# Second-layer routed output products as three float32r terms of high and low parts, in a two-layer transformer kernel

## What is computed

```python
def _L1_ffn_ref(hidden_states, router_w, w_gate_up, w_down, shared_gate_up, shared_down):
    ...
    router_logits = x @ router_w.T
    topk_vals, topk_ids = jax.lax.top_k(router_logits, top_k)      # top_k = 1, 8 experts
    gate = jax.nn.sigmoid(topk_vals.astype(jnp.float32)).astype(x.dtype)
    xs = (x[:, None, :] * gate[:, :, None]).reshape(-1, d)
    def body(acc, inp):
        wg, wd, e = inp
        h = _silu_mul(xs @ wg)                                     # silu(g) * u, each 512 wide
        o = h @ wd
        mask = (ids_flat == e)[:, None]
        return (acc + jnp.where(mask, o, jnp.zeros((), o.dtype)), None)
    ...
    shared = _silu_mul(x @ shared_gate_up) @ shared_down
    return (routed + shared).reshape(b, s, d)
```

## Time and profile before

| | |
|---|---|
| median of 3 runs | 1307.61 us (1305.98 to 1308.95) |
| the profiled execution | 1313.01 us |
| its span in the profile | 1311.2 us |
| granted TensorE clock, mean | 0.982 |
| TensorE busy | 1252.6 us (96%) |
| TensorE weight loads | 1079.0 us |
| VectorE, ScalarE, GpSimd busy | 688.8, 538.8, 668.5 us |

### The profile page before, as it was taken

One profiled execution on the slowest core, in us unless ns is written; L12 is line 12 of the kernel. 1 busy time (PEld: TensorE's weight loads), 2 busy tenths in 40 slices (PEclk: granted clock), 3 DMA queues, 4 the chain that ended last, 5 costly groups with the idle time before them and its releaser, 6 DMA issues. The chain is left out here.

```text
span 1311.2 us, 21675 instructions
## 1 busy us (share of the span) xinstructions
PE 1252.6 (96%) x7877; PEld 1079.0 (82%) x7877; DVE 688.8 (53%) x1423; ACT 538.8 (41%) x1190; POOL 668.5 (51%) x523
## 2 busy tenths in 40 slices
PE   6688999999999998999999999999999999999999
PEld 5467888888867887888788888888888887899988
DVE  6994555555676567675645434444333333433235
ACT  3675666665565333334333334333343333311122
POOL 3645778876202554576767664765545553021110
PEclk9798999999998999999999999999999999999999
DMA  9624888886705211121221112111111102799931
GB/s 317 160 53 97 175 176 183 181 176 129 177 1 161 69 53 52 61 65 49 77 69 62 36 53 69 53 38 63 53 53 36 37 25 68 273 334 336 334 126 65
DMA packets 112698, 150.70 MB, mean 115 GB/s; under 512 B 12145, under 2 KB 94193, under 8 KB 112465
## 3 DMA queue, kind: packets, MB, share of 16 engines
q1 hardware_dynamic: 96320, 123.21, 29.6%
q0 software_dynamic: 16272, 26.10, 10.5%
HBM read 121.31 MB, written 27.97 MB: 114 GB/s over the span
## 5 line engine op out<-in xcount | busy, mean ns | idle before, releaser
L1630 PE MATMUL a_p_p<-a_xr,a_wr 128*128 128x512 f32 x1152 | 308.7, 403 | 2.4 <-DVE g_x L2190 2.4
L1630 PEld LDWEIGHTS a_p_p<-a_xr,a_wr 128*128 128x128 f32 x1152 | 206.6, 189 | 42.7 <-DVE g_x L2190 3.1
L1957 POOL TENSOR_TENSOR a_sqsum<-a_sqsum,a_sq 128x512 f32<-128x512 f32 x60 | 77.8, 1297 | 232.5 <-ACT a_sq L1839 232.5
L1925 POOL TENSOR_TENSOR a_wr<-g_hold,a_wr 128x768 fp32r<-128x768 f32 x63 | 122.3, 1942 | 20.2 <-DVE a_wr L1989 20.2
L2025 DVE SCALAR_TENSOR_TENSOR a_gated<-a_th,a_p_o 128x512 f32<-128x512 f32 x64 | 44.0, 688 | 159.1 <-ACT a_sq L1839 159.1
L410 POOL DMA_INDIRECT acc<-l_ye,g_slot_token x64 | 104.5, 1632 | 39.7 <-ACT l_ye L777 19.7
L1959 POOL TENSOR_TENSOR a_gr<-a_gated,a_gr 128x512 fp32r<-128x512 f32 x64 | 97.8, 1528 | 23.7 <-DVE a_gr L2029 23.7
L1643 PE MATMUL a_p_p<-a_wvr,a_xr 128*128 128x512 f32 x384 | 108.8, 421 | 0.8 <-DVE a_xr L1983 0.8
L1701 PE MATMUL a_p_w<-a_gr,l_wo_r 128*128 128x512 f32 x384 | 100.8, 397 | 0.3 <-POOL a_gr L1959 0.3
L1685 PE MATMUL a_p_o<-a_sc,a_v 128*128 128x128 f32 x512 | 89.9, 278 | 6.6 <-DVE a_sc L2005 6.6
L1812 ACT ACTIVATE a_qk<-a_p_p 128x512 f32<-128x512 f32 x64 | 38.2, 597 | 141.0 <-PE a_p_p L1630 141.0
(11 more groups left out here) (292 smaller groups left out, 2790.7 us busy)
## 6 DMA issues: line engine op xcount, KB each, us to landing
g_hold<-in_Wqkg SPq DMA_DIRECT2D x64, 384.0 KB, 3.2
e_up<-in_gate_up SPq DMA_DIRECT2D x23, 1024.0 KB, 7.4
g_hold<-in_gate_up SPq DMA_DIRECT2D x64, 192.0 KB
e_down<-in_down SPq DMA_DIRECT2D x23, 512.0 KB, 5.9
g_hold<-in_Wv SPq DMA_DIRECT2D x16, 512.0 KB, 4.3
l_down<-in_down SPq DMA_DIRECT2D x64, 96.0 KB
acc<-l_zero SPq DMA_DIRECT2D x2, 2176.0 KB, 12.7
rows<-l_zero SPq DMA_DIRECT2D x1, 2955.5 KB, 26.9
```

The source lines that it names most:

```text
L1630: mm = pe.matmul(dst[:, :], wr[n % 2][:, wp, kk, c * P:(c + 1) * P], xr[n // H1 % 2][:, xp, kk, :], start=(kk, xp, wp) == (0, 0, 0), stop= ...
L1925: pool.tensor_tensor(wr[n % 2][:, 1, :, :], w[n % 2], wr[n % 2][:, 0, :, :], ALU.subtract).then_inc(w_parts, 1)
L1957: pool.tensor_tensor(sqsum[b % 2][:, :], sqsum[b % 2][:, :], sq[a % 2][:, :], ALU.add).then_inc(summed, 1)
```

## The change

The routed tiles' output product is computed in the three terms too.

- `hT` becomes a pair of float32r buffers, high and low, for each of its two places. VectorE writes the product of SiLU and up product to `prod`, ScalarE copies it to the high part (`high_hidden`), VectorE subtracts for the low part.
- `down` of each tile is split into `dr`, which lies in `sT[1]`, half of it for even and half for odd tiles. ScalarE makes the high part (`high_part`), GpSimd the low part (`low_part`). Both wait for the output product of tile t - 2, which read that half before.
- `output` has 12 instructions with float32r operands in place of 4 products in float32 (8 instructions), and waits for `part_low` instead of for `down`'s load.
- The shared unit of group 1 waits until the last routed output products have read `sT[1]`.

```diff
-        hT = [m.sb(f"hT{s}", [P, HC, P]) for s in range(2)]
+        hT = [[m.sb(f"hT{s}{i}", [P, HC, P], F32R) for i in range(2)] for s in range(2)]
...
+        dr = [[sT[1][i][:, 2 * s:2 * s + 2, :].rearrange("p a (b n) -> p (a b) n", n=D) for i in range(2)] for s in (1, 0)]
...
         @block.gpsimd
         def _(pool):
+            def low_part(t):
+                pool.wait_ge(part_high, t + 1)
+                if t >= 2:
+                    pool.wait_ge(y_done, Y["r", t - 2, 0] + 1)
+                pool.tensor_tensor(dr[t % 2][1], down[t % WR][:, :, :], dr[t % 2][0], ALU.subtract).then_inc(part_low, 1)
+
+            low_part(0)
             for t in range(RT1):
+                if t + 1 < RT1:
+                    low_part(t + 1)
                 pool.wait_ge(y_kept, Y["r", t, 0] + 1)
...
             def output(t):
                 y = Y["r", t, 0]
                 pe.wait_ge(h_ready, U["r", t, 0] + 1)
-                pe.wait_ge(down_in[t % WR], 16 * (t // WR + 1))
+                pe.wait_ge(part_low, t + 1)
                 pe.wait_ge(y_kept, y - 2)
-                for c in range(HC):
-                    mm = pe.matmul(p_y[y % 3][:, 0:D], hT[t % 2][:, c, :], down[t % WR][:, c, :], start=c == 0, stop=c == HC - 1)
+                terms = list(itertools.product(range(HC), ((0, 0), (0, 1), (1, 0))))
+                for n, (c, (a, b)) in enumerate(terms):
+                    mm = pe.matmul(p_y[y % 3][:, 0:D], hT[t % 2][a][:, c, :], dr[t % 2][b][:, c, :], start=n == 0, stop=n == len(terms) - 1)
                 mm.then_inc(y_done, 1)
...
+            def high_part(t):
+                act.wait_ge(down_in[t % WR], 16 * (t // WR + 1))
+                if t >= 2:
+                    act.wait_ge(y_done, Y["r", t - 2, 0] + 1)
+                act.activation(dr[t % 2][0], down[t % WR][:, :, :], ACT.Copy).then_inc(part_high, 1)
+
+            def high_hidden(u, t):
+                act.wait_ge(prod_ready, u + 1)
+                if t >= 2:
+                    act.wait_ge(y_done, Y["r", t - 2, 0] + 1)
+                act.activation(hT[t % 2][0][:, :, :].rearrange("p c n -> p (c n)"), prod[u % 2][:, :], ACT.Copy).then_inc(prod_high, 1)
+
             def high_prod(u, group, f):
-                act.wait_ge(prod_ready, group * HC + f + 1)
+                act.wait_ge(prod_ready, u + 1)
+                if group == 1:
+                    act.wait_ge(y_done, Y["r", RT1 - (1 if f >= 2 else 2), 0] + 1)
...
                 if what == "s":
                     high_prod(u, t, f)
+                else:
+                    high_hidden(u, t)
+                    if t + 1 < RT1:
+                        high_part(t + 1)
...
                 if u == 3:
                     act.activation(wd[0][:, :, :], shared_down, ACT.Copy).then_inc(down_high, 1)
+                    high_part(0)
...
                 dve.wait_ge(gate_ready, u + 1)
                 dve.wait_ge(u_done, u + 1)
+                dve.tensor_tensor(prod[u % 2][:, :], gate[u % 2][:, :], p_u[u % 2][:, :], ALU.mult).then_inc(prod_ready, 1)
                 if what == "s":
-                    dve.tensor_tensor(prod[u % 2][:, :], gate[u % 2][:, :], p_u[u % 2][:, :], ALU.mult).then_inc(prod_ready, 1)
-                    dve.wait_ge(prod_high, t * HC + f + 1)
-                    dve.tensor_tensor(sT[t % 2][1][:, f, :], prod[u % 2][:, :], sT[t % 2][0][:, f, :], ALU.subtract).then_inc(h_ready, 1)
+                    high, low = (sT[t % 2][i][:, f, :] for i in range(2))
                 else:
-                    if t >= 2:
-                        dve.wait_ge(y_done, Y["r", t - 2, 0] + 1)
-                    dst = hT[t % 2][:, :, :].rearrange("p c n -> p (c n)")
-                    dve.tensor_tensor(dst, gate[u % 2][:, :], p_u[u % 2][:, :], ALU.mult).then_inc(h_ready, 1)
+                    high, low = (hT[t % 2][i][:, :, :].rearrange("p c n -> p (c n)") for i in range(2))
+                dve.wait_ge(prod_high, u + 1)
+                dve.tensor_tensor(low, prod[u % 2][:, :], high, ALU.subtract).then_inc(h_ready, 1)
```

More of the change, by code:

```diff
@@ L1130, in experts1 @@
         (x_in_psum, xT_ready, g_done, u_done, gate_ready, h_ready, y_done, y_kept,
-         routed_added, y_stored, up_high, up_low, down_high, down_low, cols_high, cols_low, prod_ready, prod_high) = (m.sem(n) for n in (
-            "x_in_psum", "xT_ready", "g_done", "u_done", "gate_ready", "h_ready", "y_done", "y_kept", "routed_added", "y_stored", "up_high", "up_low", "down_high", "down_low",
+         routed_added, y_stored, part_high, part_low, up_high, up_low, down_high, down_low, cols_high, cols_low, prod_ready, prod_high) = (m.sem(n) for n in (
+            "x_in_psum", "xT_ready", "g_done", "u_done", "gate_ready", "h_ready", "y_done", "y_kept", "routed_added", "y_stored", "part_high", "part_low", "up_high", "up_low", "down_high", "down_low",
             "cols_high", "cols_low", "prod_ready", "prod_high"))
```

## The result

| | before | with the change |
|---|---|---|
| median of 4 runs each | 1307.57 us | 1331.26 us |
| ratio to before, 95% interval | | 1.0174 (1.0151 to 1.0196) |
| the profiled execution, its span | 1313.01, 1311.2 us | 1330.48, 1328.7 us |
| from the experts' first product to the end | 198.9 us | 223.4 us |

The change made the kernel slower by 23.7 us; 19.4 were forecast. The last row of the table is read from the profiles: the experts' first product starts at 1112.33 us of the span before, and at 1105.31 after. The parts ahead of it are the same program and took 7 us more in the profiled execution of before. The experts alone grew by 24.5 us, and that is what the profiles are compared by.

The account below looks back on a forecast made before the run. TensorE was taken to set the pace in the routed tiles. From the profiled 1313.0, +20.0 for waits and -0.6 for two output products gave 1332.4; the median, 5.4 lower, 1327.0 us. Forecast's own range 1324 to 1332, whole range 1321 to 1338.

Parts of the forecast that it names:

- The output product: TensorE's routed output product: 12 instructions in 1.44 us instead of 8 in 1.73, 0.29 us less per tile.
- VectorE's sequence: Routed tiles: VectorE's wait for ScalarE's copy and a subtraction move the xT copy's start from +0.92 to +2.31 us.
- The restart: TensorE's gate product starts 0.51 us after the xT copy starts; gate and up products then take 3.65 us.
- The period: Time from one routed tile to the next: 2.82 + 3.65 = 6.47 us, 0.95 more than 5.52.
- How often: The gate products of tiles 2 to 22 wait: 21 x 0.95 = +20.0 us.
- ScalarE: ScalarE's added copies in routed tiles, 0.63 and about 1.05 us: the weights' copy delays no SiLU, no cost.
- The loads: Routed tiles' down weights: landing takes 5.5 to 7.1 us, there by +2.3, in time for ScalarE's copy.
- GpSimd: GpSimd's added weight subtraction, 2.43 us per routed tile, ends by +7.6 or +8.0, before VectorE's at +8.11: no cost.
- rival 2: TensorE's clock falls: a third of 21 tiles run hidden products at half clock, +25 us, 1352; chance 0.04.
- Rival 1: VectorE's low hidden subtraction collides with GpSimd's, waiting 1.2 us in each of 21 tiles: +25, 1352; chance 0.08.
- Rival 3: Faster: VectorE's sequence fits behind TensorE's work if the xT copy starts by +1.15: -6.7 us, 1300.9; chance 0.04.
- Rival 4: The 12 output products are as slow per instruction as the 8, 2.6 us; time within 2 us of forecast; no chance given.

Follow-up runs that it names:

- both moves: The changed kernel with VectorE's keep_x(t + 1) ahead of the wait for ScalarE's high part and its columns' subtraction one tile later: 1301.93 us, ratio 0.9966.

## Why the prediction was right, and where it was short

*What bounds the kernel*: right. The chain holds TensorE and its wait alone, and the experiment with the float32 products shows that TensorE's own 0.3 us count for nothing as long as the wait ends last.

*The output product*, 1.44: measured 1.42 to 1.44.

*VectorE's sequence*, `xT` copy at +2.31: measured +2.33. ScalarE's hand-overs are 0.72 and 0.67, as in the shared units. *The restart*, 0.51 and 3.65: measured 0.52 and 3.64. One look at tile 1 was enough. *The period*, 6.47: measured 6.49. (TensorE's wait, 1.16 in the forecast, reads 1.04 in the chain. I had taken 1.66 from the chain, where a piece begins at the modelled end of the one before it, and 2.82 from the timeline's starts, which lie 0.16 earlier; the period doesn't depend on it.) *How often*, 21: right, and moving `keep_x` takes it back in one step.

*ScalarE*: right that it cost nothing; with `keep_x` ahead of the wait all its copies are still there and the period is 5.23. *The loads*: between 1145 and 1250 us `down` landed in 3.3 to 5.1 us, where before took 4.5 to 7.1. With both moves, at a period of 5.23, it is 5.0 to 7.0 again, so it goes with the period.

*GpSimd*: right for the subtraction of a usual tile, which runs from +4.34 to +6.74 (1199.48 to 1201.88 in the profile). The step that was mis-sized is what stands around it. I counted VectorE's two-input subtraction in `times` against GpSimd's and showed that they miss each other; in tile 0, which I had put at no cost, they met, and it did cost nothing. The columns' subtraction of tiles 2, 5 and 8 also has both inputs in SBUF, and I looked at those tiles for ScalarE only. It starts at about +3.9, during GpSimd's scatter and 0.4 ahead of its subtraction. Three times 0.97 us, 2.9 in all, are missing from my sum for that; with it 1330 would have stood there. The Trainium skill's rule ("SBUF — State Buffer", "SBUF: two separate sides") covers both, and this case's traces agree with it that one of the two waits: 3.88 against 1.22. I applied it to one pair of instructions where the rule speaks of every such pair. The rule also says that whichever starts first goes first; by the starts in the rows that is not so in these three tiles, as the last section shows.

*The clock* (rival 2, 0.04) came once, for 1.6 us in the profiled execution, right after a gap of 2.0 us that the columns had made; two more such gaps passed without it. With gaps of 1.0 us in each tile (the columns one tile later) it did not come. With ScalarE's copy twice 20 gaps of 1.6 us passed and it came after the one of 1.99; with GpSimd's subtraction twice it came five times, after gaps of 1.82 to 2.53. A chance of 0.04 for a fall in a third of the tiles was not too low for gaps of 1.0, but a single fall belonged into the forecast's own range. That 1331.26 still lies in that range, 1324 to 1332, is partly luck: nothing in it stood for the columns or for a fall.

*Rival 1* had the right mechanism and the wrong place. *Rival 3*'s condition was stated correctly: with `keep_x` ahead of the wait the period is 5.23. *Rival 4* could not be told from the time, and the trace excludes it.

In the first of the listed periods (6.84), at tile 1, VectorE's product starts 0.62 after the transposes instead of 0.27. It does so in the other changed kernels too, also in those with `keep_x` ahead of the wait, except in the one with ScalarE's copy twice, where the same 0.62 stands once at a later tile, in the period of 9.02. The kernel before doesn't have it. Its cause stays open; it is worth 0.35 us.

## What to carry to other kernels

When an engine takes over part of another's work, look at what stands behind the new wait in the queue, not at the engine's busy share: VectorE was busy for 30% of the stage, and a wait and a subtraction of together 1.4 us ahead of an `xT` copy cost 20 us. Put what the bounding engine needs next ahead of every wait that it doesn't depend on; here two lines moved turned +23.7 into no change, and with the second move into 5.2 us less than before. And when GpSimd gets long instructions, list every two-input SBUF operation of VectorE in the stretch, the rare ones too.

## What the runs showed of the hardware that I had not expected

VectorE's two-input subtraction delays GpSimd's scatter too. In the profile of before, 20 of the 23 scatters take 0.96 to 1.02 us; the other three are those that start 0.36 us after a columns' subtraction, and take 1.7. Two rows of before show one of them:

```profile
1163.42 1.22 DVE L1395 TENSOR_TENSOR e_cr<-g_hold,e_cr 128x1024 fp32r<-128x1024 f32 x1
1163.78 1.69 POOL L1206 DMA_INDIRECT out<-e_ye,e_token  x1 [4.56 <-DVE e_ye L1373]
```

Who goes first can't be told from the starts alone. In the changed kernel, in all three tiles that split columns, VectorE's columns' subtraction starts first, at 1142.61 in the tile shown, during a scatter, and GpSimd's subtraction 0.41 later, when the scatter is over. Yet GpSimd's runs in its usual 2.39 us, and VectorE's ends 1.08 after it. With ScalarE's copy twice VectorE's starts 0.13 into the scatter and 0.87 ahead of GpSimd's subtraction, and there VectorE's takes 1.22 and the scatter 0.97, their usual times, and GpSimd's subtraction is the one that is longer. That the two subtractions keep each other out is shown; whether a scatter holds VectorE up, and why VectorE lost its turn in the one kernel and not in the other, is not.
